# Two chained cross-attentions on one core: small tensors moved so that the large ones start at multiples of 512 bytes

## What is computed

```python
def _L0_xattn_ref(emb, latent, Wq, bq, Wk, bk, Wv, bv, gamma, beta):
    q = jnp.einsum('bte,ef->btf', emb, Wq) + bq           # emb 32x256x512
    k = jnp.einsum('bml,le->bme', latent, Wk) + bk        # latent 32x256x256
    v = jnp.einsum('bml,le->bme', latent, Wv) + bv
    w = jax.nn.softmax(jnp.einsum('bte,bme->btm', q, k) * scale, axis=1)
    x = jnp.einsum('btm,bme->bte', w, v) + emb
    mu, var = jnp.mean(x, -1, keepdims=True), jnp.var(x, -1, keepdims=True)
    return (x - mu) * jax.lax.rsqrt(var + EPS) * gamma + beta

def _L1_xattn_ref(query, key, Wq, bq, Wk, bk, Wv, bv, Wo, bo):
    Q, K, V = (query @ Wq + bq), (key @ Wk + bk), (key @ Wv + bv)
    weights = jax.nn.softmax(jnp.einsum('bqh,bkh->bqk', Q, K) * scale, axis=-1)
    return query + (weights @ V) @ Wo + bo

x = _L0_xattn_ref(x, ctx_512, ...)
x = _L1_xattn_ref(x, ctx_512, ...)
```

## Time and profile before

| | us |
|---|---|
| median of 3 runs | 705.82 (705.16 to 706.65) |
| the profiled execution | 704.28 |
| its span, first to last instruction | 702.2 |
| TensorE busy | 681.6, 97% |
| VectorE, GpSimd, ScalarE busy | 517.1, 488.8, 430.5 |
| HBM traffic | 49.5 MB, 70 GB/s |

### The profile page before, as it was taken

One profiled execution on the slowest core, in us unless ns is written; L12 is line 12 of the kernel. 1 busy time (PEld: TensorE's weight loads), 2 busy tenths in 40 slices (PEclk: granted clock), 3 DMA queues, 4 the chain that ended last, 5 costly groups with the idle time before them and its releaser, 6 DMA issues.

```text
span 702.2 us, 12504 instructions
## 1 busy us (share of the span) xinstructions
PE 681.6 (97%) x4107; PEld 595.1 (85%) x4107; DVE 517.1 (74%) x1235; ACT 430.5 (61%) x1040; POOL 488.8 (70%) x391
## 2 busy tenths in 40 slices
PE   8987999999999999999999999999999999999967
PEld 7864888988898898889888888888889888988856
DVE  4999586776868687777858677685868767686845
ACT  2654567576665757667565757666575766757432
POOL 0367868779495877859586876949587785955680
PEclk9999999999999999999999999999999999999999
DMA  8801104040220404031030404012040403101003
GB/s 303 296 1 37 54 1 151 1 150 0 71 79 0 149 0 149 0 114 35 23 127 0 149 0 149 0 58 91 0 149 0 149 0 102 47 6 55 1 1 120
DMA packets 30336, 49.50 MB, mean 70 GB/s; under 512 B 2160, under 2 KB 10352, under 8 KB 30320
## 3 DMA queue, kind: packets, MB, share of 16 engines
q1 hardware_dynamic: 30320, 49.29, 20.7%
HBM read 32.51 MB, written 16.78 MB: 70 GB/s over the span
## 4 chain that ended last, share of the span: by engine, by line
PE 89%; DVE 6%; POOL 2%; issue 1%; ACT 1%; DMA 1%; SPq 0%; DVEq 0%; POOLq 0%
PE bank L392 76%; PE bank L399 12%; DVE n L839 1%; PE bank L412 1%; DMA wk_sb<-in_L_xattn_Wk_dram 1%; DVE rb L928 1%; POOL x_even L1194 1%; POOL wq_sb L1158 1%; DVE n L1006 1%; POOL wq_sb L1154 1%; DVE stats L995 0%; DVE xT_lo L815 0%; POOL rstd L1164 0%; DVE x_even L990 0%; POOL prod L1171 0%
## 5 line engine op out<-in xcount | busy, mean ns | idle before, releaser
L1171 POOL TENSOR_TENSOR prod<-n,u_b 128x512 f32<-128x512 f32 x64 | 81.6, 1294 | 40.3 <-DVE n L1006 40.3
L813 DVE SCALAR_TENSOR_TENSOR y_lo<-bank,terms,y_hi 128x512 fp32r<-128x512 f32 x64 | 46.3, 750 | 77.6 <-ACT y_hi L637 77.6
L637 ACT ACTIVATE y_hi<-bank,terms 128x512 fp32r<-128x512 f32 x64 | 44.1, 689 | 56.3 <-PE bank L392 56.1
L1164 POOL TENSOR_TENSOR rstd<-var_eps,minus_half 128x2 f32<-128x2 f32 x32 | 22.3, 698 | 77.3 <-DVE var_eps L1002 77.2
L1210 POOL TENSOR_TENSOR r<-r,beta_b 128x512 f32<-128x512 f32 x60 | 75.8, 1296 | 0.0
L1203 POOL TENSOR_TENSOR r<-n,gamma_b 128x512 f32<-128x512 f32 x60 | 75.1, 1279 | 0.0
L639 ACT ACTIVATE pc_hi<-bank 128x512 fp32r<-128x512 f32 x32 | 19.1, 597 | 68.5 <-PE bank L392 68.5
L392 PE MATMUL bank<-nT_hi,wqk_hi 128*128 128x512 f32 x128 | 51.3, 401 | 3.0 <-DVE nT_lo L815 3.0
L979 DVE SCALAR_TENSOR_TENSOR r<-bank,rinv,r 128x512 f32<-128x512 f32 x60 | 44.7, 747 | 12.8 <-PE bank L392 12.8
L392 PE MATMUL bank<-xT_hi,wqk_hi 128*128 128x512 f32 x128 | 52.1, 407 | 2.0 <-DVE xT_lo L815 2.0
L392 PE MATMUL bank<-wv_hi,wc_hi 128*128 128x512 f32 x128 | 52.1, 407 | 1.7 <-issue 1.7
(11 more groups left out here) (197 smaller groups left out, 2358.1 us busy)
## 6 DMA issues: line engine op xcount, KB each, us to landing
out_dram<-r SPq DMA_DIRECT2D x15, 1024.0 KB, 5.0
x_even<-in_x_dram SPq DMA_DIRECT2D x8, 1024.0 KB, 7.1
ctxn<-in_ctx_dram SPq DMA_DIRECT2D x16, 512.0 KB, 3.6
x_odd<-in_x_dram SPq DMA_DIRECT2D x8, 1024.0 KB, 6.9
wq_sb<-in_L_xattn_Wq_dram SPq DMA_DIRECT2D x4, 256.0 KB, 3.2
wk_sb<-in_L_xattn_Wk_dram SPq DMA_DIRECT2D x2, 512.0 KB, 6.5
wv_sb<-in_L_xattn_Wv_dram SPq DMA_DIRECT2D x2, 512.0 KB, 8.9
wq_sb<-in_L_xattn_Wq_dram SPq DMA_DIRECT2D x1, 1024.0 KB, 11.4
```

The source lines that it names most:

```text
L637: i = act.activation(dst, at((name, k))[:], ACT.Identity, bias=bias)
L813: i = dve.scalar_tensor_tensor(dst, src, bias, high.bitcast(F32), ALU.add, ALU.subtract)
L1164: pool.tensor_tensor(rstd[:, q], var_eps[:, q], minus_half[:, q], ALU.pow).then_inc(rstd_ready, 1)
L1171: pool.tensor_tensor(prod[j % 2][:], N[:, j, :], u_b[1][:], ALU.mult).then_inc(prod_ready, 1)
```

## The change

Twelve small tensors (16 to 28 bytes each, 32 as allocated) move from three places to a place between `ones_r` and the weights. Twelve further ones move from the middle to the end, behind `R`. No instruction of any engine is changed; all tensors keep their shapes and names. In these lines `...` marks what is left out.

```diff
         ident = sb("ident", [P, P])
         ones_r = sb("ones_r", [P, P], F32R)
+        terms = [sb("terms0", [P, KD + KC + 1]), sb("terms1", [P, KD + KC + 1])]
+        ccol = [t[:, KD:KD + KC + 1] for t in terms]
+        gamma_col, bv1_col = sb("gamma_col", [P, KD]), sb("bv1_col", [P, KD])
+        gscale = sb("gscale", [P, KD])
+        rs, r0, r0s = sb("rs", [P, J]), sb("r0", [P, J]), sb("r0s", [P, J])
+        neg0, sum0, rinv0 = (sb(n, [P, J]) for n in ("neg0", "sum0", "rinv0"))
+        r1 = sb("r1", [P, J])
+
         WQK = [pair("wqk0", [P, KD, C]), pair("wqk1", [P, KD, C])]
         WV0 = pair("wv0", [P, KC, D])
         WVO = pair("wvo", [P, KC, D])

-        terms = [sb("terms0", [P, KD + KC + 1]), sb("terms1", [P, KD + KC + 1])]
-        ccol = [t[:, KD:KD + KC + 1] for t in terms]
...
-        gamma_col, bv1_col = sb("gamma_col", [P, KD]), sb("bv1_col", [P, KD])
-        gscale = sb("gscale", [P, KD])
...
-        rs = sb("rs", [P, J])
...
-        r0 = sb("r0", [P, J])
-        r0s = sb("r0s", [P, J])
         RB = sb("rb", [P, J * P])
         bias = [prod[0][:], prod[1][:], bias2[:], RB[:]]
-        neg0, sum0, rinv0 = (sb(n, [P, J]) for n in ("neg0", "sum0", "rinv0"))
-        r1, r1s, negmx1, neg1, sum1, rinv1 = (sb(n, [P, J]) for n in ("r1", "r1s", "negmx1", "neg1", "sum1", "rinv1"))
-        stats = sb("stats", [P, J, 6])
-        mv = sb("mv", [P, J, 2])
-        var_eps = sb("var_eps", [P, J])
-        rstd = sb("rstd", [P, J])
-        waited = sb("waited", [P, 2])
-        minus_half = sb("minus_half", [P, J])
         CT_even, CN_even = pair("cT_even", [P, KC, J * P]), pair("cn_even", [P, J, C])
...
         E1 = sb("e1", [P, 2, RT, M])
         R = sb("r", [P, J, D])
+        r1s, negmx1, neg1, sum1, rinv1 = (sb(n, [P, J]) for n in ("r1s", "negmx1", "neg1", "sum1", "rinv1"))
+        stats = sb("stats", [P, J, 6])
+        mv = sb("mv", [P, J, 2])
+        var_eps = sb("var_eps", [P, J])
+        rstd = sb("rstd", [P, J])
+        waited = sb("waited", [P, 2])
+        minus_half = sb("minus_half", [P, J])
```

## The result

The changed kernel takes 699.9 us (median of 6 runs, 697.5 to 701.1); the kernel before took 706.1 us in the same session (6 runs, 705.2 to 708.0). The ratio is 0.991, 95% interval 0.9896 to 0.9923: 0.9% faster. The forecast of 706.6 us was wrong, and the time lies in the range, 4 us above the rival "one step lower".

What follows compares the result with a forecast made beforehand. TensorE was taken to bound the kernel, with no slack in the loop passes. Terms of -0.4 + 0.7 + 0.5 = +0.8 us on a profiled 704.3 gave 705.1, plus 1.5 for the median: 706.6 us, range 685 to 717.

Steps and rivals of the forecast that it cites:

- one step lower: Rival: 512-column matmul starts settle 6.67 ns lower, at 226.7 ns, 10 us, 696 us; with 256 columns too, 687; chance 0.20.
- The bound: Loop passes: TensorE busy 40.23 of 40.23 us, no other engine within 10 us; time is matmul count times start distance.
- The price without a loss: fp32r matmuls without a loss, read from plain fp32: 217 ns for 512 columns and 109 ns for 256.
- the swapped pairs: nT moves 416 over weights at 128, wv 128 over 416; they differ by 0.3 ns, taken as showing addresses don't matter.
- the only pair with equal residues: cT with y1, 256 columns, both operands at 416 modulo 512, running at exactly 120.0 ns, the longest of its size.
- the one put at 233 ns for the 512 columns: 1536 matmuls of 512 columns taken to stay at 233 ns, only the 384 of xT falling 1 ns: -0.4 us.
- The hole: No pair in the trace has both operands on a boundary of 64 bytes, so 0, 0 pairs were unseen.
- The 256-column term: All 1536 matmuls of 256 columns come to 120.0 ns: y with cT +0.7 us, w and pt with cn +0.5 us.
- One step higher: Rival: both streams collide and 512-column starts settle at 240 ns, 10.3 us slower, 717 us; chance 0.17.
- the loss goes: Rival: misalignment causes the whole loss of 16 and 10 ns per matmul, which vanishes: 40 us, 666 us; chance 0.12.
- The two rules: Skill rules: 16-byte line crossings make the change worth nothing, 705.8 us; N / 2.4 + 2.5 ns gives 216 and 109 ns.

Runs made afterwards that it cites:

- the bare stream: A kernel of independent fp32r matmuls alone, the kernel's whole computation left out; with one moving column read repeatedly, 215.8 ns at 512 columns and 111.7 at 256.
- the map: Matmuls alone, computation left out, at pairs of moving and stationary starts in 32-byte steps; 512 columns: 226.7 ns at equal starts, 231.7 to 234.3 at most others.

## Why the prediction was wrong

**The bound was right.** The pass is TensorE alone in both kernels, 39.80 of 39.80 us, and none of the other engines' groups that the page shows moved by more than 1.7%. What the matmul starts lost, the time lost.

**The price without a loss was right.** 217 and 109 ns were read from plain fp32; the bare stream with one moving column gave 215.8 and 111.7, the second 2.7 above. So there is a loss of 17.5 ns at 512 columns, and the change took 6.6 of it.

**The failed step** is the argument from the swapped pairs: "Equal costs speak for a loss that belongs to the fp32r stream and not to the address." nT and wv cost the same 233, one with the moving operand at 416, the other with the stationary one there. I took it that neither place matters, because I asked only about each operand's own place. The two pairs are at distances +32 and -32, and the map has 233.3 at both. A quantity that depends on the pair gives equal costs to swapped pairs without being free of the address. Had I written the distances beside the rows, I would have seen that no 512-column pair of the trace had distance 0, and that cT with y1, which did, ran at an even 120.0 without jitter: a sign of a settled rhythm and not of a collision. (The prediction calls it the only pair with equal residues; by its own list w with cn and pt with cn, 416 and 416, are two more.) The term that failed is the one put at 233 ns for the 512 columns: it measured 226.7 settled. The hole was named (no pair with both sides on a boundary of 64), but as a hole in alignment; it was one in distance.

**The 256-column term was right**, for its own reason: the relation of residues decides, y with cT went from 118.2 to 120.0 and all kinds stand at 120.0. Sized at +0.7 and +0.5 us, it measured 48 ns a pass, 0.7 us in all.

**The rival "one step lower" is what happened**, for 512 columns and not for 256. Its step of 6.67 ns gave 226.7, and 226.7 it is; also the 113.3 that it named for 256 columns exists, at other distances. Its pass was 39.6 us; the sum took all 96 matmuls of a pass as settled, which is 96 x 6.6 = 634 ns. The means above give 473 ns, as the six stretches of a pass (xT, nT, three of wv, wvo) begin with three to five longer steps, and 48 ns more went into the 256 columns: 39.60 + 0.16 + 0.05 = 39.81, and 39.80 was measured. So it said 696 and the kernel took 700. Its number was in part luck, for its premise, that streams settle only on multiples of 6.67 ns, doesn't hold: 228.9, 231.7, 116.7 and 117.8 are settled means too, some of them of unequal steps (226, 229, 232). I gave it 0.20 since "the one equal pair sits at its upper value"; that is true of 256 columns, and the two sizes don't share a best distance.

**"One step higher" and "the loss goes" fell.** Nothing reached 240 when settled. The remaining 11 ns above 215.8 stayed at every pair of starts that was tried.

**The two rules weighed.** The rows first: operands all on 32-byte multiples went from 233 to 226.7 ns by their places alone. The Trainium skill, page "SBUF — State Buffer", section "Specifications (TRN2)", counts crossings into 16-byte lines; by it the change would be worth nothing. The measurement decides: what happened here is not covered by that rule. The Trainium skill, page "TensorE: Matmul & The Clock Gate", section "Back-to-back issue gap", with 216 ns for 512 columns, agrees with the 215.8 of the stream that reads one moving column, and with no stream here that reads a whole moving tensor in fp32r. The same section of the Trainium skill gives that formula for an isolated matmul, and 131 ns at 512 columns for a stream with weight loads, which the prediction left out; no fp32r stream of 512 columns here went below 215.8.

**Proportion.** A single half-clock stretch of 6.8 us cost 2.4 us in the profiled execution, over a third of the gain of 6.2. The pass length, in both kernels the same in every pass of the 13 to 0.01 us, showed the effect where the total hid half of it.

## What to carry to other kernels

Where TensorE streams fp32r without waits, read the distance between starts, not durations, and tabulate moving start minus stationary start modulo 256 for every kind of pair, beside its ns. Give each size its own best distance (here 0 for 512 columns, -64 for 256) by placing small tensors as spacers; "aligned to 512" is only one way to make pairs equal, and a few small tensors put in the wrong place (192 bytes here) take nearly all of the gain away unnoticed. This is shown for fp32r with 128 stationary columns and starts on multiples of 32 bytes; with 64 or 32 stationary columns other distances were the cheap ones. An argument from two equal costs holds only for causes that differ between the two.

## What the runs showed of the hardware that was not expected

- The two operands of fp32r matmuls interact by address: with 128 stationary columns the settled spacing goes by (moving start - stationary start) modulo 256 on the 32-byte grid, 226.7 to 234.3 ns at 512 columns and 113.3 to 120.0 at 256, and at some distances by the entry as well. Plain fp32 (429.2 and 215.8) and a moving operand of one column (215.8 and 111.7) don't depend on it.
- The spacings are rhythms with memory: at 512 columns and distance 0 the first five or so of each stretch mostly are longer (224 to 236, mean 232), and at distance -64 with 256 columns the entry picks 113.3 or 117.8 for the whole stretch, at +64 with 512 columns 228.9 or 233.3. What in the chip sets them, no run showed.
- Starts off the grid by 4, 20 or 36 bytes cost up to 237.8 ns; by 16 bytes they can help at 256 columns (113.3 where the grid has 117.8) and hurt at 512 (230 to 233 for 226.7, at equal starts).
- A bare fp32r stream of 128 or of 192 columns takes 111.3 to 111.7 ns a matmul, as much as the 256-column one with a single moving column; 320, 384 and 448 columns take 146.7, 173.3 (175.8 at one pair) and 200 to 207. So the 111.7 at 256 columns may be a floor that has nothing to do with the moving operand; no run tells.
